# Routing the first half of the batches one step earlier, and turning its first expert rows inside step 15

## The reference

```
x = layernorm(x + scan(x @ B.T, decay A) @ W.T + b)                  # "mixing": U, Y
x = layernorm(x + cross_attention(x, ctx; 16 heads of 16, rotary, |q-k| <= 50))   # K, Q, V, scores, O
# experts: 16 experts, each takes its best 64 of the 256 tokens of each batch
probs = softmax over tokens of  silu(x @ router_w1) @ router_w2      # one row per (batch, expert)
weights, tokens = top_k(probs, 64); weights /= sum
out[tokens] += weights * ((silu(x[tokens] @ w1[e]) * (x[tokens] @ w2[e])) @ w3[e])
x = layernorm(x + out)
```

## Time and profile before

| | |
|---|---|
| median of 3 runs | 1072.29 us (1072.12 to 1074.49) |
| the profiled execution: its time | 1073.45 us |
| its span | 1071.5 us |
| mean granted TensorE clock | 0.977 |
| busy: PE, PEld, DVE, ACT, POOL | 93%, 79%, 68%, 55%, 63% |
| steps 15 and 16 of mixing (PE's first head of step 15 to the end of its last gather) | 435.8 to 476.1 us |
| first expert product | 476.58 us |

### The profile page before, as it was taken

The page is one execution under the profiler, slowest core; times in us unless marked ns, Lnnn a source line. Parts: engine busy times, 40 slices in busy tenths (PEclk is TensorE's granted clock), DMA queues, the critical chain, the costliest instruction groups (busy, mean ns, idle before and its releaser), DMA issues.

```text
span 1071.5 us, 21268 instructions
## 1 busy us (share of the span) xinstructions
PE 994.0 (93%) x6436; PEld 846.8 (79%) x6436; DVE 732.3 (68%) x2176; ACT 587.6 (55%) x1226; POOL 674.4 (63%) x785
## 2 busy tenths in 40 slices
PE   4699999999999999879999999999999999999990
PEld 3577887777778777658788888888888888888880
DVE  4578888888887798758554777465656665665634
ACT  1155555555575556556656656565555557555541
POOL 5456666666666566368756665776767667676533
PEclk9899999999999999899999999999999999999995
DMA  6333443334433332525576666666686666756646
GB/s 191 81 99 98 103 105 102 101 100 103 102 100 93 89 78 70 190 94 168 128 232 135 161 138 161 135 162 138 159 219 158 150 161 138 166 139 157 158 79 181
DMA packets 114998, 142.57 MB, mean 133 GB/s; under 512 B 15184, under 2 KB 88144, under 8 KB 114768
## 3 DMA queue, kind: packets, MB, share of 16 engines
q1 hardware_dynamic: 87600, 106.62, 34.4%
q0 software_dynamic: 24576, 33.57, 18.1%
q10 hardware_dynamic: 2720, 1.17, 0.5%
HBM read 90.71 MB, written 29.36 MB: 112 GB/s over the span
## 4 chain that ended last, share of the span: by engine, by line
PE 52%; DVE 1%; DMA 1%; issue 1%; ACT 0%; POOL 0%; DVEq 0%; POOLq 0%; SPq 0%; ACTq 0%
PE gate_bank L1349 16%; PE attn L1349 16%; PE value_bank L1349 16%; PE turn_bank L1359 2%; DMA last<-acc_rows 1%; DVE stats L1620 0%; DMA acc_rows<-y,slots_now 0%; DVE last L1631 0%; PE attn L1433 0%; DVE hidden L1613 0%; PE attn L1406 0%; ACT y L1510 0%; ACT h_hi L1500 0%; DVE mv L1624 0%; ACT w_hi L1483 0%
## 5 line engine op out<-in xcount | busy, mean ns | idle before, releaser
L1290 POOL DMA_INDIRECT acc_rows<-y,slots_now x128 | 205.6, 1606 | 136.5 <-issue 73.4
L1613 DVE TENSOR_TENSOR hidden<-gate,value_bank 128x512 f32<-128x512 f32 x128 | 87.9, 687 | 154.0 <-ACT gate L1496 150.5
L945 DVE CUSTOM_DVE_ANT_0 scored<-score,band 128x178 f32<-128x178 f32 x512 | 150.0, 337 | 62.8 <-PE score L589 58.6
L787 ACT ACTIVATE probsT<-scoreT 128x356 f32<-128x356 f32 x256 | 117.6, 467 | 137.3 <-PE scoreT L618 111.3
L1496 ACT ACTIVATE gate<-gate_bank 128x512 f32<-128x512 f32 x128 | 76.6, 598 | 184.5 <-PE value_bank L1349 179.1
L1349 PE MATMUL attn<-w_hi,h_hi 128*128 128x256 f32 x512 | 146.0, 285 | 0.2
L1349 PE MATMUL attn<-w_hi,h_lo 128*128 128x256 f32 x512 | 143.2, 280 | 0.0
L1349 PE MATMUL attn<-w_lo,h_hi 128*128 128x256 f32 x512 | 143.2, 280 | 0.0
L589 PE MATMUL score<-k_stack,q_stack 96*128 96x178 f32 x512 | 124.1, 325 | 7.4 <-DVE nmax L945 4.3
L589 PEld LDWEIGHTS score<-k_stack,q_stack 96*128 96x128 f32 x512 | 88.9, 194 | 37.4 <-DVE nmax L945 18.1
L618 PE MATMUL scoreT<-q_stack,k_stack 97*128 97x356 f32 x256 | 117.0, 458 | 0.0
(11 more groups left out here) (213 smaller groups left out, 2376.9 us busy)
## 6 DMA issues: line engine op xcount, KB each, us to landing
arena<-in_w SPq DMA_DIRECT2D x96, 512.0 KB
k_stack<-high_k SPq DMA_DIRECT2D x128, 64.0 KB, 2.2
q_stack<-high_q SPq DMA_DIRECT2D x128, 64.0 KB, 2.3
arena<-in_xT SPq DMA_DIRECT2D x16, 256.0 KB, 2.8
arena<-in_x SPq DMA_DIRECT2D x16, 256.0 KB, 3.2
arena<-in_cT SPq DMA_DIRECT2D x16, 256.0 KB, 3.6
k_stack<-low_k SPq DMA_DIRECT2D x64, 64.0 KB, 2.2
q_stack<-low_q SPq DMA_DIRECT2D x64, 64.0 KB, 2.2
```

What stands on the lines that cost most here:

```text
L787: nc.scalar.activation(probsT[g % 2][:, u % HG, :, :].rearrange("p a s -> p (a s)"), scoreT[u % 2][:, 0:2 * SPAN], ACT.Exp, scale=1.0 / DH ...
L945: op = nc.vector.tensor_tensor_reduce(scored[t % 2][:, q, :], score[t % 2][:, q * SPAN:(q + 1) * SPAN], band[:, q, :], -1.0, BIG, ALU.add, ...
L1290: nc.gpsimd.indirect_dma_start(dram["acc"][c], bass.IndirectOffsetOnAxis(ap=now[:, m:m + 1], axis=0), y[m][:], None, compute_op=ALU.add).t ...
L1613: nc.vector.tensor_tensor(hidden[f % 2][:], gate[f % 2][:], value_bank[f % 2][:], ALU.mult).then_inc(hidden_ready, 1)
```

## The change

The whole router of batches 0 to 7 is moved one step ahead. Silu goes from (10, 9) to (10, 8); logits and maximum from step 11 to step 10; exponential and scaling from step 12 to 11; the eight rounds to two each in steps 11, 12, 13 and 14; `weigh_picked` to (14, 15); the turn of the picks to (15, 1), in the other work bank's place "K"; `place_picked` to (15, 2). POOL takes the row numbers and issues the four gathers near the start of its step 15 (after `bias_residual`), ahead of `inverse_sums` and `inverse_deviation`. PE turns the rows in step 15, half at slot 8 and half at slot 11, both into work bank "X", each ahead of the next slot's head; DVE splits them at slots 9 and 12. New waits: PE's O waits for `route.placed` (the picks lie in its bank), PE's slot 8 and 11 for the gathered rows, its second turn and OX for DVE's split, and DVE's split for `turned_heads` of batch 14. The wait for `scored_ready` of the drain goes. The arithmetic is the same.

```diff
@@ POOL step
                 if it.batch(0):
                     bias_residual(it)
+                if it.fixed and it.i == NB - 1:
+                    pool.wait_ge(route.placed, 1)
+                    nc.gpsimd.tensor_copy(keep["rows_now"][0][:], keep["row_of"][:, 0, 0:NC2 // 2]).then_inc(rows_taken, 1)
+                    pool.wait_ge(rows_taken, 1)
+                    pool.wait_ge(x2_kept, 16 * (NB // 2) + 1)
+                    for m in range(NC2 // 2):
+                        nc.gpsimd.indirect_dma_start(
...
(the same lines go from the end of the step)
@@ PE step
                         if n == 0:
                             begin(it, "O")
+                            if it.fixed and it.i == NB - 1:
+                                pe.wait_ge(route.placed, 1)
...
                         pe.wait_ge(x2_ready, it.lin(1, -1))
+                        if it.fixed and it.i == NB - 1:
+                            pe.wait_ge(xT_lo_ready, KT)
                         transposed(it, "OX", x2cur)
-                    if only(it, 11, t, 13):
+                    if only(it, 10, t, 13):
...
-                    if only(it, NB - 1, t, 10):
+                    if only(it, NB - 1, t, 1):
                         pe.wait_ge(route.picked, 1)
-                        picks = begin(it, "R")
+                        picks = begin(it, "K")
...
-                    if only(it, NB, t, 5):
-                        pe.wait_ge(rows_in[0], 16 * CB)
-                        pe.wait_ge(scored_ready, NH * NB)
-                        for k in range(KT):
+                    for k in range(KT):
+                        if only(it, NB - 1, t, 8 + 3 * k):
+                            turn = begin(it, "X")
+                            pe.wait_ge(rows_in[0], 16 * CB)
+                            if k:
+                                pe.wait_ge(xT_lo_ready, k)
                             for m in range(CB):
-                                mm = nc.tensor.transpose(score[k][:, m * P:(m + 1) * P],
+                                mm = nc.tensor.transpose(turn[:, m * P:(m + 1) * P],
...
-                        if it.fixed and it.i == 11:
+                        if it.fixed and it.i == 10:
                             pe.wait_ge(logits_kept, 1)
-                        if it.fixed and it.i == NB - 1:
-                            pe.wait_ge(route.placed, 1)
@@ ACT step
-                    if only(it, 10, t, 9):
+                    if only(it, 10, t, 8):
...
-                    if only(it, 12, t, 1):
+                    if only(it, 11, t, 1):
@@ DVE step
-                    if only(it, 11, t, 14):
+                    if only(it, 10, t, 14):
...
-                    if only(it, 12, t, 2):
+                    if only(it, 11, t, 2):
...
-                    for n, (i, at) in enumerate(((12, 7), (12, 14), (13, 1), (13, 14), (14, 1), (14, 14), (15, 1), (15, 4))):
+                    for n, (i, at) in enumerate(((11, 7), (11, 14), (12, 1), (12, 14), (13, 1), (13, 14), (14, 1), (14, 14))):
...
-                    if only(it, 15, t, 7):
+                    if only(it, 14, t, 15):
                         weigh_picked(dve, route)
...
-                    if only(it, NB, t, 6):
-                        for k in range(KT):
+                    for k in range(KT):
+                        if only(it, NB - 1, t, 9 + 3 * k):
+                            dve.wait_ge(scoreT_ready, NH * (NB - 1))
                             dve.wait_ge(keep["rows_turned"], k + 1)
-                            nc.vector.tensor_copy(keep["xT_hi0"][:, k, :], score[k][:]).then_inc(xT_hi_ready, 1)
-                        for k in range(KT):
+                            nc.vector.tensor_copy(keep["xT_hi0"][:, k, :], bank("X")[:]).then_inc(xT_hi_ready, 1)
                             dve.wait_ge(xT_hi_ready, k + 1)
-                            nc.vector.tensor_tensor(keep["xT_lo0"][:, k, :], score[k][:], keep["xT_hi0"][:, k, :],
+                            nc.vector.tensor_tensor(keep["xT_lo0"][:, k, :], bank("X")[:], keep["xT_hi0"][:, k, :],
                                                     ALU.subtract).then_inc(xT_lo_ready, 1)
                     if it.fixed and it.i == NB - 1:
-                        if t == 12:
+                        if t == 2:
```

More of the change, by code:

```diff
@@ L503, in step @@
                     bias_residual(it)
+                if it.fixed and it.i == NB - 1:
[5 more added lines that the diff above has]
+                        nc.gpsimd.indirect_dma_start(
+                            keep["rows"][0][:, m, :], None, dram["x2"][0],
+                            bass.IndirectOffsetOnAxis(ap=keep["rows_now"][0][:, m:m + 1], axis=0)).then_inc(rows_in[0], 16)
                 if there(it, "U"):
```

## The result

The changed kernel takes 1081.04 us (median of 7 runs, 1078.74 to 1086.21), the kernel before 1072.29 us (7 runs, 1067.99 to 1074.49). The ratio is 1.0093, 95% interval 1.0073 to 1.0114: 0.9% slower, where 0.3% was forecast. The profiled execution has a span of 1081.3 us, 9.8 more than before's 1071.5.

A forecast was written before the change was run, and what follows sets the result against it. PE's chain of waits up to the beginning of experts was taken as the bound. Steps 10 to 13 +0.8, step 15 +5.0 and drain -2.3 sum to +3.5 us on 1072.3: 1075.8 us, range 1070 to 1079.5.

The forecast's parts named there:

- the mechanism in step 15: Step 15: PE waits at slot 8 for the gathered rows and OX for the second split; +5.0 us.
- The drain: Step 16: the wait for rows and eight transposes go, x2 is late next; -2.3 us, bounds -1.5 and -3.6.
- Steps 10 to 13: Router a step earlier: step 11 becomes a step with two rounds, +0.8 us; the earlier silu 0.
- The rows' landing: Step 15: last gather issued by 447.4, rows there at 451.2 us, 452.3 at worst, because SP's queue has the engines.
- PE behind the rows: Step 15: four transposes, heads(9) and the turn's start take 1.1 us; turned head at 452.3 in place of 448.58, +3.7 us.
- The second split: Step 15, slot 12: DVE splits the second half behind x2 and the scores, OX waits for it; +1.7 us.
- Behind the drain: From the beginning of experts on: nothing is touched, so the change is worth nothing later.
- A: Step 15: engines take POOL's packets in turn with SP's, rows land at 449.2; +1.6 us, 1073.9 us; chance 0.18.
- B: Step 15: the pause is short and the clock does not fall; -4.5 us, 1067.8 us; chance 0.13.
- C: Gathers get in front of maxima and weights, a second wait follows the first; +7.6 us, 1079.9 us; chance 0.05.
- The forecast's upper end: Rows at 452.3 us in step 15 and a drain that gives 1.5 us; sum +5.4 us.

The follow-up runs named there:

- e5: Kernel before with only the router a step earlier; gathers stay at the end of POOL's step 15, turn and split in the drain: 1072.75 us, ratio 0.9999.
- e2: Changed kernel with SP's four accumulator copies issued one after each of steps 11 to 14, not behind the weight loads: 1078.45 us, ratio 1.0044.
- e8: e2 with SP's three weight loads also held until the gathered rows are in: 1076.55 us, ratio 1.0044.
- e10: Changed kernel with the rows' second half turned into the other work bank, so OX waits only for the first split: 1080.72 us, ratio 1.0065.
- e7: Changed kernel with the two row turns at slots 11 and 12 of step 15, not 8 and 11: 1079.25 us, ratio 1.0074.
- e9: Changed kernel with 7 extra products that nobody reads on PE in step 16, where e4 has 17: 1080.00 us, ratio 1.0073.
- e1: Changed kernel with only the turn and split of the first rows put back to step 16; routing, picks and gathers stay early: 1072.39 us, ratio 0.9998.
- e6: e1 with the accumulator copies issued one after each of steps 11 to 14, as in e2: 1071.00 us, ratio 0.9982.
- e4: Changed kernel with 17 extra products that nobody reads on PE in step 16, ahead of OX and R: 1082.20 us, ratio 1.0082.
- e3: Kernel before with only SP's four accumulator copies issued one after each of steps 11 to 14: 1071.03 us, ratio 0.9987.
- e11: e6 with four extra products that nobody reads, two each ahead of OX and R in the drain: 1071.25 us, ratio 0.9994.

## Why the prediction was wrong

The direction was right, and so was the mechanism in step 15, where two sizes were too small. The drain, forecast at -2.3 us, gave nothing: there the prediction left out what the new pauses do to the clock. The profile's +9.8 us is -0.9 + 8.15 + 0 + 2.6, the forecast's +3.5 was 0.8 + 5.0 - 2.3 + 0. In the order of the prediction:

**Steps 10 to 13, +0.8 us.** Not seen: e5 has 0.9999, and the changed kernel reached step 14's x2T at 433.3, before at 434.2. The interval of e5, 0.9981 to 1.0016, and the spread of the early part are too wide to exclude 0.8 us. The silu a slot earlier did only change the place of PE's wait, as was said: 2.8 us in step 10, 2.7 before.

**The rows' landing: the first term that was mis-sized.** The gathers ended at 445.5 where 447.4 was said, since the first one began at 440.6 and not at 441.4 and took 1.19 us and not 2.24; the rows came at 452.9 where 451.2 was said. So the landing took 7.4 us behind the last gather, where 3.8 was taken and 4.9 was the worst case. The second profile of the changed kernel has 7.3. The bound came from the whole trace's scatters, none of which had these seven 512-KB transfers of SP's ahead. e2 (landing 4.7 us, three copies away) and e8 (landing 1.9 us, loads away too) take it apart: with both away nothing is left of the excess. Counted from x2T of step 14, the rows are 2.6 us later than forecast (19.6 us, not 17.0).

**PE behind the rows.** From the rows to OX 10.25 us, where the prediction's terms give 9.4 (457.2 + 3.7 - 0.35 - 451.2). From the rows to the turned head it was 1.46 us, said 1.1: the clock was at 0.50 and the four transposes took 1.08 us, where 0.6 was taken. The second split was in front of OX as forecast (e10: 1.6 to 1.9 us, said 1.7). With R 0.36 us nearer to OX, step 15 is +8.15 us, said +5.0: 2.6 of the 3.15 us are the later rows.

**The drain, -2.3 us: the step that failed in kind.** The chain was read rightly: OX came 9.2 us behind the first turned head of the drain, 1.75 us sooner than before's 10.9. But the prediction took the pause away, asked what is late next, and counted the clock only as a gain: the half clock behind the old pause would go, 0.5 us. It did not ask what the pauses that are left do to it. Before, the wait of 2.63 us was one pause, the half clock behind it fell on the row turns and heads, and R and the first expert products ran at 2.4 GHz. With the turns gone, three pauses of 1.52, 1.18 and 1.15 us stand in a row, and the clock is at 1.2 GHz from OX to the first products: what OX gained, 1.75 us, is lost again, 7.4 us from OX to experts where there were 5.7. The other profiles with this drain agree (R to experts 17.53 in the second of the changed kernel, 17.5 in e2, e7 and e10, 17.6 in e8). In e9, with PE's pauses part filled, R to experts is 15.4 us, -2.2. In e1, where the eight turns stay in the drain but need not wait, it is 15.3 and 15.7, with pauses of 1.18 and 1.43 us left in the first; e6's 16.8 shows that this does not hold every time.

**Behind the drain, 0.** It was +2.6 us in the profile: 1.0 in unit 0, which e9 and e1 don't have, and 1.6 behind unit 3's wait for x2. That wait is 2.2 to 2.3 us in every version; what differs is the clock in the 4.4 us behind it:

| profile | clock, first 2.6 us of experts | clock behind unit 3's wait | experts to the end, us |
|---|---|---|---|
| before, twice | 1.00, 1.00 | 1.00, 1.00 | 594.9, 595.5 |
| changed, twice | 0.59, 0.61 | 0.61, 0.61 | 597.5, 597.3 |
| e9, e4 (PE busy in the drain) | 1.00, 1.00 | 1.00, 1.00 | 594.9, 595.4 |
| e1, twice | 1.00, 1.00 | 1.00, 1.00 | 595.0, 595.1 |
| e3 (before, copies early) | 1.00 | 0.61 | 596.5 |
| e11, twice | 1.00, 1.00 | 0.61, 0.70 | 597.3, 597.3 |
| e10 | 0.50 | 1.00 | 596.2 |

So both parts repeat in the changed kernel, and both are gone when the drain is held at full clock (e9, e4). But the second also comes without the change's waits (e3) and with a drain at full clock (e11), so why the clock falls in unit 3 stays open.

**The rivals.** A, the engines taking turns: refuted by 7.4 us of landing. From 448 to 450 us SP's queue had 46 packets and POOL's 42, so POOL's did get in between, and still they were not done before SP's copies were. The rule of the Trainium skill (DMA: Bandwidth & Descriptors, Queues, rings and completion order), that an engine goes from queue to queue packet by packet, agrees with these counts; what the prediction drew from it, rows 1.8 us behind the last gather, does not hold. A likely reason, which no run takes apart, is that a turn lasts as long as the neighbour's packet: the copies' had 2.02 MB in 176, 11.5 KB each, and POOL's 0.09 MB in 42, 2 KB each. B did not occur; C's second wait is in e8, not in the changed kernel. The forecast's upper end joined rows at 452.3 with a drain that still gave 1.5 us. With a drain of 0 the same sum is 0.8 + 6.1 = +6.9, 1079.2 us, still short of the measured time: the landing beyond its bound and the loss behind the drain are needed as well.

**What stays open.** e1 and e11 have 2.0 and 3.5 us less than the kernel before from x2T to experts in the mean of two profiles, and their medians show 0.1 and 1.2 us. For e11 the table above has where it went: behind the first product it takes 2.1 us more than the kernel before, which leaves 1.4. For e1 nothing is given back there, and its interval reaches down to 0.9982, 1.9 us; whether it gains anything is open. The runs of one kernel lie 6 to 10 us apart where there are ten or more of them, more than any of these effects. e6, 0.9982, is the lowest ratio of the versions that were run; e3, e11 and e1 overlap with it, and with eleven intervals one that just misses 1 is weak evidence.

## What to carry to other kernels

Work that is moved "where a bank is free" must be checked against the transfers that are in flight there: here four gathers, 0.5 MB together, were there 1.9 us behind the last issue in a quiet stretch and 7.4 us behind it with seven big transfers ahead, and a wait on them in the middle of a busy step dragged the whole step. Put the wait where the rows are long there (e1: 1.0093 became 0.9998), and keep big copies that nobody waits for away from transfers that somebody does wait for (e2: 1.0044).

When a stall is removed from a drain, redo the sum with the clock: where short pauses are left over in a row, PE may fall to half clock on work that had been at full clock.

## What the runs showed that I had not expected

Taking work away slowed the work behind it: OX to experts took 5.7 us before and 7.4 with the row turns gone. Seven extra products that nobody reads brought it to 5.1 (e9). R to experts repeated to 0.1 us in the changed kernel (17.53 twice) and, with four extra products and the turns, in e11 (15.30 and 15.29).

A 4-KB transfer held PE for 1 to 2.4 us: the maxima's wait was 2.24 and 2.40 us before, between 1.07 and 2.06 in four profiles with copies moved away, and came up at another slot (1.98 us) when the weight loads were moved.

The same wait of 2.2 us, in unit 3, was followed by full clock in some versions and by half clock in others, and each of the four versions with two profiles fell on the same side both times.
